# Selecting the 32 nearest of 64 through two sorted halves and a threshold, in a windowed-attention block on one core

## The reference

```python
diff = k_windows - q_h[:, :, None, :]
dist = jnp.sqrt((diff * diff * m_h).sum(axis=-1) + 1e-08)
dist = jnp.where(mask[None], dist, jnp.inf)
neg_d, loc = jax.lax.top_k(-dist, K)          # K = 32 of 64
infl = jnp.exp(-topd)                         # topd = -neg_d
infl = infl / (infl.sum(axis=-1, keepdims=True) + 1e-08)
context = jnp.einsum('btk,btkd->btd', infl, neighbor_v)
context = context + gate * 0.1 * heb_ctx      # a small per-head matrix on q / |q|
outs.append(q_h * context)
```

## Time and profile before

| | |
|---|---|
| median of three runs | 865.25 us (864.89 to 867.82) |
| the profiled execution | 865.7 us, span from first to last instruction 863.9 us |
| TensorE busy | 764.0 us, 88%; mean granted clock 0.895 of full speed |
| VectorE busy | 795.0 us, 92% |
| ScalarE busy | 620.0 us, 72% |
| GpSimd busy | 461.4 us, 53% |
| match_replace, all | 2048, 400.5 us, with 2048 value loads |
| max, all | 2048, 280.4 us |

### The profile page before, as it was taken

How to read it: one execution, slowest core, us unless ns; L and a number is a source line. 1 busy time by engine, 2 the same in 40 slices (tenths; PEclk the granted TensorE clock), 3 DMA queues, 4 the chain that set the end, 5 groups by cost and what they waited for, 6 DMA issues and landing times.

```text
span 863.9 us, 21621 instructions
## 1 busy us (share of the span) xinstructions
PE 764.0 (88%) x4885; PEld 500.8 (58%) x4885; DVE 795.0 (92%) x6746; ACT 620.0 (72%) x1862; POOL 461.4 (53%) x870
## 2 busy tenths in 40 slices
PE   5987999998899999888989988999889898989975
PEld 3444556565566665556666655666556666655644
DVE  5865999799999998999999999979999999999890
ACT  3982466687777876777877787668777777877763
POOL 1113455565556665556666665556555565666442
PEclk9995777799999987999999999779999999998775
DMA  5300000010000000011001110001010100110000
GB/s 164 106 21 16 23 18 25 21 30 28 29 29 29 26 27 27 29 30 30 25 28 30 31 30 28 28 21 31 27 30 29 30 30 23 31 31 29 23 9 10
DMA packets 49233, 27.27 MB, mean 32 GB/s; under 512 B 5513, under 2 KB 48593, under 8 KB 49105
## 3 DMA queue, kind: packets, MB, share of 16 engines
q1 hardware_dynamic: 49104, 25.90, 10.1%
HBM read 10.28 MB, written 4.19 MB: 17 GB/s over the span
## 4 chain that ended last, share of the span: by engine, by line
DVE 75%; PE 17%; ACT 3%; issue 2%; DMA 2%; POOL 1%; SPq 0%; POOLq 0%; ACTq 0%
DVE work L939 39%; DVE m L929 26%; DVE key L955 4%; PE psC L1167 2%; PE psD L1112 2%; PE psW L1183 2%; PE psD L1012 2%; PE psD L1104 1%; DVE den L972 1%; DMA big<-in_x 1%; PE psW L1185 1%; PE psW L1194 1%; PE psW L1136 1%; PE psX L1119 1%; PE psC L1095 1%
## 5 line engine op out<-in xcount | busy, mean ns | idle before, releaser
L939 DVE MATCH_REPLACE8 work<-m,work 128x64 f32<-128x64 f32 x1536 | 300.6, 204 | 0.0
L929 DVE MAX8 m<-work 128x8 f32<-128x64 f32 x1536 | 210.2, 205 | 0.0
L471 POOL TENSOR_TENSOR big<-work,con 128x512 f32<-128x512 f32 x128 | 161.7, 1286 | 21.5 <-ACT work L617 21.5
L1167 PE MATMUL psC<-vst,big 128*128 128x34 f32 x1024 | 139.6, 282 | 0.0
L1167 PEld LDWEIGHTS psC<-vst,big 128*128 128x128 f32 x1024 | 125.2, 193 | 17.1 <-issue 2.1
L450 POOL TENSOR_TENSOR hsc<-gat,rnn 128x8 f32<-128x8 f32 x64 | 13.0, 204 | 222.4 <-ACT rnn L699 222.4
L1136 PE MATMUL psW<-con,big 128*128 128x128 f32 x512 | 92.2, 309 | 27.8 <-POOL big L471 19.5
L939 DVE MATCH_VALUE_LOAD work<-m,work 128x8 f32 x1536 | 113.0, 74 | 0.0
L1136 PEld LDWEIGHTS psW<-con,big 128*128 128x128 f32 x512 | 62.5, 155 | 64.7 <-POOL big L471 46.7
L939 DVE MATCH_REPLACE8 work<-m,key 128x64 f32<-128x64 f32 x512 | 99.9, 203 | 0.0
L676 ACT ACTIVATE key<-key,bias 128x512 f32<-128x512 f32 x64 | 46.2, 722 | 55.2 <-DVE key L955 55.2
(11 more groups left out here) (204 smaller groups left out, 1630.9 us busy)
## 6 DMA issues: line engine op xcount, KB each, us to landing
hst<-hT_all SPq DMA_DIRECT2D x64, 96.0 KB
tst<-qT_all SPq DMA_DIRECT2D x256, 17.0 KB
big<-in_x SPq DMA_DIRECT2D x16, 256.0 KB, 2.8
xs<-in_x SPq DMA_DIRECT2D x64, 64.0 KB, 1.9
out<-yo SPq DMA_DIRECT2D x64, 64.0 KB, 1.6
sst<-nst SPq DMA_DIRECT2D x128, 3.0 KB
tst<-nst SPq DMA_DIRECT2D x128, 2.0 KB
con<-in_consts SPq DMA_DIRECT2D x1, 549.5 KB, 5.4
```

The source lines that it names most:

```text
L471: nc.gpsimd.tensor_tensor(wun[:, s, heads].rearrange("p h (v j) -> p h v j", v=2), work[:, s].rearrange("p (h j) -> p h j", h=NH)[:, heads ...
L929: last = v.max(m8[:, h], src[:, h * WIN:(h + 1) * WIN])
L939: last = v.match_replace(work[:, s, cols], m8[:, h], src[:, cols], GONE)
L1167: last = mm(pC[:, h * 2 * VD:(h + 1) * 2 * VD], wts[:, s, h], vst[:, s4, h].rearrange("p v e -> p (v e)"), start=True, stop=True)
```

## The change

The chunks, the stages and the layout of engines stay. What changes:

- **Distances.** The mask and product for a head are 160 columns wide (block before, 32 columns of q, own block); the two halves of a chunk are separate matmuls into partitions 0 to 63 and 64 to 127 (16 matmuls per chunk instead of 8; a float32 matmul is two instructions in the trace). One relu over 128 partitions replaces two over 64.
- **Selection.** VectorE works on the squared distances themselves. The 64 candidates of a head are paired, j with j+32: the minima of the pairs go to `low_high[:, 0]`, the maxima, negated, to `low_high[:, 1]`. Of each set of 32 the 16 largest are found in order (`pick`, `drop`, `pick`). Of two such lists `meet` takes the larger of one and the negated other, position by position, and `theta` is the minimum over positions: the threshold, which is the 33rd smallest distance.
- **Keep mask.** GpSimd subtracts (`diff` = key - theta, 512 elements), TensorE transposes `diff`, ScalarE takes two signs of it (with +1e-30 and -1e-30), and TensorE multiplies them with `count_bf`, a matrix that also counts equal distances ahead of a candidate, so that ties are resolved by position. VectorE multiplies (count >= -16) with the weights (`wsel`).
- **Weights.** TensorE transposes `key`, ScalarE takes log, exp(0.5 x), exp(-x) in the transposed layout (`infl`). GpSimd splits `wsel` by two masks (`wab`, two instructions of 512), which TensorE uses directly. The eight transposes of weights and the two copies `wts` go.
- **Values** are computed per block of 64 tokens and kept in `vst` for a batch; the copy of `hT_all` by DMA (`hst`) goes.
- **Order.** GpSimd: `diff`, `n_c` (moved from ScalarE), `sqs`, `sst`, `gat`, the mixing (four wide instructions instead of five), `wab`. One stage more in depth (i runs to 67). `keep_clock`, L1165 and `n2g` go; `selm` is computed once.

The diff, cut to its core:

```diff
-GONE = -1e4
+GONE = -3e38
+KEEP = -16.0
@@ gpsimd
-            def step(i, ph):
-                k, s, s4 = i - 2, ph % 2, (ph - 2) % 4
...
+            def step(i):
+                k = i - 1
+                if there(k):
+                    pool.wait_ge(theta_ready, k + 1)
+                    need(pool, dT_ready, k)
+                    nc.gpsimd.tensor_tensor(diff.rearrange("p (h j) -> p h j", h=NH),
+                                            key[:, k % 2].rearrange("p (h j) -> p h j", h=NH),
+                                            theta[:, k % 2].unsqueeze(2).broadcast_to([P, NH, WIN]),
+                                            ALU.subtract).then_inc(diff_ready, 1)
...
+                    nc.gpsimd.tensor_scalar(n_c[:, k % 2], x2[:, k % 2], nm_c[:, k % 2:k % 2 + 1], rs_c[:, k % 2:k % 2 + 1],
+                                            ALU.add, ALU.mult).then_inc(nc_ready, 1)
...
+                    nc.gpsimd.tensor_tensor(sqs[:], win, win, ALU.mult).then_inc(opnd_ready, 1)
...
+                    nc.gpsimd.tensor_tensor(t1[:].rearrange(h3, h=NH), cst[:, s, :, 0:HD],
                                             rden[:, s].unsqueeze(2).broadcast_to([P, NH, HD]), ALU.mult).then_inc(mix_step, 1)
...
+                k = i - 1
+                if there(k):
+                    pool.wait_ge(w_ready, k + 1)
+                    need(pool, c_ready, k - 1)
+                    for v, part in enumerate((of_own, of_before)):
+                        nc.gpsimd.tensor_tensor(wab[:, k % 2, v].rearrange("p (r t) -> p r t", r=4),
+                                                wsel.rearrange("p (r t) -> p r t", r=4),
+                                                part.unsqueeze(1).broadcast_to([P, 4, CH]), ALU.mult).then_inc(wab_ready, 1)
@@ scalar
+                    nc.scalar.activation(fst[:, 0], pDT, ACT.Sign, bias=bias[:, 4:5]).then_inc(f_ready, 1)
+                    nc.scalar.activation(fst[:, 1], pDT, ACT.Sign, bias=bias[:, 5:6]).then_inc(f_ready, 1)
...
+                    nc.scalar.activation(e, pXT, ACT.Ln, bias=bias[:, 1:2]).then_inc(ln_done, 1)
+                    act.wait_ge(ln_done, k + 1)
+                    nc.scalar.activation(e, e, ACT.Exp, scale=0.5).then_inc(root_done, 1)
+                    act.wait_ge(root_done, k + 1)
+                    nc.scalar.activation(e, e, ACT.Exp, scale=-1.0).then_inc(infl_ready, 1)
@@ vector
+            def pick(rnd, u):
+
+                where = slice(8 * rnd, 8 * rnd + 8)
+                for h in range(NH):
+                    last = v.max(top[:, u, h, where], low_high[:, u, h])
+                last.then_inc(picked, 1)
+
+            def drop(u):
+
+                for h in range(NH):
+                    last = v.match_replace(low_high[:, u, h], top[:, u, h, 0:8], low_high[:, u, h], GONE)
+                last.then_inc(picked, 1)
...
+                    v.tensor_tensor(low_high[:, 1], x4[:, :, 0], x4[:, :, 1], ALU.max).then_inc(pair_done, 1)
+                    v.tensor_tensor(low_high[:, 0], x4[:, :, 0], x4[:, :, 1], ALU.min).then_inc(pair_done, 1)
+                    dve.wait_ge(pair_done, 3 * i + 1)
+                    v.tensor_scalar(low_high[:, 1], low_high[:, 1], -1.0, None, ALU.mult).then_inc(pair_done, 1)
...
+                    v.scalar_tensor_tensor(out=e, in0=pB, scalar=0.0, in1=e, op0=ALU.max, op1=ALU.min).then_inc(d2_ready, 1)
...
+                    v.scalar_tensor_tensor(out=wsel, in0=pZ, scalar=KEEP, in1=infl[:, k % 2], op0=ALU.is_ge,
+                                           op1=ALU.mult).then_inc(w_ready, 1)
...
+                    v.scalar_tensor_tensor(out=meet, in0=top[:, 1], scalar=-1.0, in1=top[:, 0], op0=ALU.mult,
+                                           op1=ALU.max).then_inc(meet_done, 1)
+                    dve.wait_ge(meet_done, i + 1)
+                    need(dve, diff_ready, i - 1)
+                    v.tensor_reduce(theta[:, i % 2], meet, AX_X, ALU.min).then_inc(theta_ready, 1)
@@ tensor
+                    for r in range(4):
+                        last = nc.tensor.transpose(pDT[:, r * P:(r + 1) * P], diff[:, r * P:(r + 1) * P], ident)
+                    last.then_inc(dT_ready, 1)
...
+                    mm(pZ, count_bf[:, 0], fst[:, 0], start=True, stop=False)
+                    mm(pZ, count_bf[:, 1], fst[:, 1], start=False, stop=True).then_inc(count_ready, 1)
...
+                        for late in range(2):
+                            toks = slice(late * WIN, (late + 1) * WIN)
+                            last = mm(bank_of(r)[toks, g, 0:PW], tst[strip, s, g, toks], sst[strip, s, g, late * B0:late * B0 + PW],
+                                      start=False, stop=(g == NG - 1), skip_group_check=True)
-            def keep_clock(bank, times):
```

More of the change, by code:

```diff
@@ L54, in constants @@
     before = np.where(j > i, 0.0, BIG)
[L56 to L59, removed]
+    c[:, C_MASK:C_MASK + PW] = np.concatenate([before, np.zeros((P, QW)), own], 1)
+    slot = (np.arange(P) % WIN)[:, None]
+    tok = (np.arange(CH) % WIN)[None, :]
+    c[:, C_OWN:C_OWN + CH] = slot <= tok
+    c[:, C_OWN + CH:C_OWN + 2 * CH] = slot > tok
     e = np.arange(P) % 32
@@ L75, in constants, with counting, adaln_block @@
     return c
-def adaln_block(nc, x, encq, encv, w1, b1, w2, b2, base, hebu, hebv, dec, wr, amat, bmat, cin, wmod, consts, out):
+def counting():
+    jp, j = np.arange(WIN)[:, None], np.arange(WIN)[None, :]
+    eye, after = (jp == j).astype(np.float32), (jp >= j).astype(np.float32)
+    below, equal = 97.0 * eye - 1.0, 33.0 * eye - after
+    m = np.zeros((P, 2, P), np.float32)
+    for a in range(2):
+        rows = slice(a * WIN, (a + 1) * WIN)
+        m[rows, 0, rows] = 0.5 * (equal - below)
+        m[rows, 1, rows] = -0.5 * equal
+    return m
+def adaln_block(nc, x, encq, encv, w1, b1, w2, b2, base, hebu, hebv, dec, wr, amat, bmat, cin, wmod, consts, counts, out):
     ctx = ExitStack()
@@ L149, in adaln_block @@
         bsc = big[:].rearrange("p a s (b d) -> p (a s) b d", b=NB)
-        hst = sb("hst", [P, 2, 3 * WIN])
         tst = sb("tst", [P, 2, NG, CH])
         sst = sb("sst", [P, 2, NG, SW])
[L154 to L160, removed]
+        sqs = sb("sqs", [P, NG, 3 * WIN])
+        nst = sb("nst", [2 * NH, 2, 3 * WIN])
+        selm = sb("selm", [P, NB, NG, 2 * NH])
+        low_high = modn_all[:, 0:NH * WIN].rearrange("p (u h j) -> p u h j", u=2, h=NH)
+        top = gsgn_all[:].rearrange("p u (h n) -> p u h n", h=NH)
+        meet = gabs_all[:, 0].rearrange("p (h n) -> p h n", h=NH)
+        theta = sb("theta", [P, 2, NH])
+        diff = wmod_sb[:, 0:NH * WIN]
+        fst = sb("fst", [P, 2, 4 * CH], BF16)
+        infl = z8_all[:, 0:8 * CH].rearrange("p (s x) -> p s x", s=2)
+        wab = big[:, 0].rearrange("p s (v x) -> p s v x", v=2)
+        wsel = big[:, 1, 0, 0:4 * CH]
+        count_f = big[:, 1, 1, 0:2 * P]
+        vst = sb("vst", [P, NBLK, 4, VP])
         qh = sb("qh", [P, 4, NH, 2 * HD])
@@ L332, in steps, with there, new_blocks @@
                     routing(i)
-                step(i, i % 4)
-        def there(i, off):
-            return not isinstance(i, int) or 0 <= i + off < NCH
+                step(i)
+        def there(k):
+            return 0 <= k < NCH
         def column(k):
             return k * CH + (k // CPB) * WIN
+        def new_blocks(k):
+            c = k % CPB
+            return [2 * c + n for n in range(3) if n or c == 0]
         block = ctx.enter_context(nc.Block())
@@ L491, in step @@
[L491 to L496 removed]
+                    pool.wait_ge(mix_step, 4 * k + 4)
+                    nc.gpsimd.tensor_tensor(osp[:, s].rearrange(h3, h=NH), t1[:].rearrange(h3, h=NH), q,
+                                            ALU.mult).then_inc(osp_ready, 1)
@@ L506, in routing @@
                     pool.wait_ge(pG_ready, 2)
-            steps(pool, step, routing)
+            steps(step, routing)
         @block.scalar
@@ L727, in _ @@
+                k = i + 3
+                if there(k):
+                    act.wait_ge(pnn_ready, k + 1)
+                    need(act, gat_ready, k - 3)
+                    need(act, rnn_ready, k - 3)
+                    nc.scalar.activation(n2[:, k % 4], pNN, ACT.Copy, scale=-2.0).then_inc(n2_ready, 1)
+            steps(step, routing)
         @block.vector
```

703 lines of the change are left out of this document (360 added, 343 removed).

## The result

The changed kernel takes 991.97 us (median of 4 runs, 989.04 to 995.9), the kernel before, run beside it, 866.54: 1.144 times as long, 95% interval 1.137 to 1.151. Forecast were 907 us and a range of 750 to 950. The sign is right; the time lies 42 us outside the range.

A forecast was written before the change was run, and what follows sets the result against it. VectorE, waiting behind GpSimd for the shared port, was taken to bound the loop: start 92.5, loop 64 x 12.24 = 783.4 plus 6, tail 24, span 905.9; about 907 us, 4.8% slower, range 750 to 950.

The forecast's parts named there:

- the term for SyncE's queue: SyncE's DMA issues per step: one fewer (`hst`), nothing waits for it; no time added.
- from `key` to the next: Chain over TensorE and ScalarE between `key` instructions, 9.8 us a step, the bound if VectorE has no port stall.
- 12.24 us a step: VectorE's step in the loop with its waits behind GpSimd; 64 of them make 783.4 us.
- the forecast had allowed 6: Loop steps where TensorE is late at a slow clock: 6 us in all.
- Port stalls: VectorE's `meet`, pair maximum, minimum and negation wait behind GpSimd instructions: 3.5 us lost a chunk.
- the prediction's own balance, 11.58 us a step: Loop step at which the forecast sum equals the old kernel's time, so the change stops losing.
- VectorE's own work: VectorE per chunk without waits: 8.7 us, with 0.093 a max and 0.161 a replace with its load.
- the 11 us for swaps: ScalarE's time per chunk if each sign swapped tables; 8 us otherwise, both under 12.2.
- Start and tail: Outside the loop: start 90.5 + 2 = 92.5 us, tail 20.7 + 3.3 = 24 us.
- no port stall: Rival for the loop: VectorE not stalled, 9.8 us a step, 751 us in all; chance 0.22.
- Part of it: Rival: maximum waits for `wab`, minimum and negation slip in before `diff`; 10.6 us a step, 803 us; chance 0.14.
- TensorE becomes the bound: Rival: TensorE at 1.2 GHz, 14.5 us a chunk, about 1050 us, or 13.0 and 956; chance 0.09.

The follow-up runs named there:

- e1_rows_first: Changed kernel with SyncE issuing the norm rows before the output store: 848.71 us, ratio 0.975 to the kernel before.
- e5_store_mid: Changed kernel with the output store moved between the four `tst` loads and the norm rows on SyncE: 848.05 us, ratio 0.974.
- e6_xs_in_ring: Changed kernel with the `xs` load moved from behind the norm rows to between the store and the `tst` loads: 1032.32 us, ratio 1.184.
- b1_before_rows_first: Kernel before the change, with SyncE issuing the norm rows ahead of the store: 875.03 us, ratio 1.002.
- e9_diff_fillers_only: Changed kernel with only four unread matmuls added before TensorE's wait for `diff`, store still ahead of the norm rows: 982.32 us, ratio 1.130.
- e7_both_fillers: Changed kernel with norm rows first, two `tensor_reduce` for the pair instructions, and four unread matmuls before TensorE's wait for `diff`: 783.35 us, ratio 0.897.
- e3_fillers: Changed kernel with four unread 320-column matmuls before TensorE's wait for the norm rows: 964.09 us, ratio 1.107.

## Why the prediction failed, step by step

**The step that failed** is the term for SyncE's queue, which the prediction put at nothing: "SP issues one DMA less (`hst`); nothing waits for it" is true of `hst` and is all that it says of that queue's order. With it failed the ring "from `key` to the next" of 9.8 us. That ring was added up from TensorE and ScalarE only and closed over `key`. The real one closes over SyncE's queue, whose part alone is 6.7 us: the store 0.35, four loads 2.75, norm rows 1.18 and 1.10, the gaps between, and the landing. The rows stood in the trace of before; the prediction counted issues and didn't ask what stood first in the queue and how late it would be, though the change puts a logarithm and two exponentials, which wait for the transposes, ahead of `yo` on ScalarE. Shown: taking it out gives 143 us back (e1_rows_first, e5_store_mid), adding 0.47 us to it costs 40 (e6_xs_in_ring), and the exchange is worth nothing where there is no ring (b1_before_rows_first). The prediction had named this outcome as one that would refute it: a chain of waits that runs over ScalarE and TensorE.

**The forecast's 12.24 us a step** looks near the ring's 12.12. That is chance: the two have no term in common. What separates 907 from 992 in numbers is then the clock: 63 x (13.59 - 12.12) = 93 us, where the forecast had allowed 6. The trace bears this out: 57 x 1.60 = 91 us lie in TensorE's part of the ring. The reason for the 6 was that TensorE's busy time, 11.4 us at equal shares, fits under the step. (Its terms add up to 8.5 us or more, not 8.4, and 8.4 x 1.88 / 1.04 is 15.2, not 14.5; equal shares are then 11.8, still under 12.24. TensorE was busy for 656 / 63 = 10.4 us a step.) In a ring busy time is not the measure: each slow instruction of it lengthens the step, whatever pauses the engine has elsewhere. Once the ring is open (e1_rows_first, clock 0.83) the mean step is 0.15 us above the regular one, 10 us over the loop, about half of it in the first nine steps.

**Port stalls**: the mechanism was right, in kind and in place. With the ring open (e1_rows_first) the forecast's sequence can be read off:

```profile
406.92 0.18 DVE L1039 RECIPROCAL rden<-den 128x8 f32<-128x8 f32 x1
...
408.79 1.30 DVE L1062 SCALAR_TENSOR_TENSOR gabs_all<-gsgn_all 128x128 f32<-128x128 f32 x1
410.13 0.29 DVE L1066 TENSOR_REDUCE theta<-gabs_all 128x8 f32<-128x128 f32 x1
410.52 0.99 DVE L998 TENSOR_TENSOR modn_all<-key 128x256 f32<-128x256 f32 x1
411.44 1.26 DVE L999 TENSOR_TENSOR modn_all<-key 128x256 f32<-128x256 f32 x1
412.62 0.28 DVE L1001 TENSOR_SCALAR modn_all<-modn_all 128x256 f32<-128x256 f32 x1
```

`meet` stands behind `wab` 1, the maximum behind `wab` 2, the minimum behind `diff`. The picks start 5.9 us after `rden` (412.82), forecast were 6.87: the negation does not wait, because `n_c`, which was to stand in front of it, itself waits for ScalarE's `nm_c` and `rs_c` (it started at 412.67 there). 2.6 us are lost instead of 3.5 if the forecast's 3.3 for a free port is right (5.9 - 3.3; no run has a free port throughout), and the step is 11.23 us, not 12.24: even with all its stalls the selection is faster than the old one at 11.47. By the prediction's own balance, 11.58 us a step, the port alone would have made the change a gain. The Trainium skill ("SBUF — State Buffer", Who interferes with whom) says that on trn2 `tensor_reduce` never contends for the shared ports. By that rule the trace agrees: 693 and 680 ns for 512 elements, the rate of the earlier trace rows, beside GpSimd's work. The Trainium skill's page "VectorE: DVE Perf Modes", Rules for kernel authors, calls `tensor_reduce` the slowest operation and says to consider restructuring where it is on a hot path. Here it pays: the two take 0.69 and 0.68 us, the three instructions that they replace 0.98, 1.26 and 0.28. That is so only because of the stalls. At their shortest the three take 0.42, 0.42 and 0.28 us in the trace of the change, 1.1 in all against 1.37, so by these durations the reduces would be the slower way where nothing stalls.

**VectorE's own work**: 16 max took 1.50 us to the start of the next instruction (412.82 to 414.32 in e1_rows_first), 0.094 each (0.093 forecast), a replace with its load 0.16 (0.161). Both terms were right. **ScalarE**: a sign takes 0.69 to 0.70 us, and the trace has only three table loads, none of them in the loop; the 11 us for swaps did not come. **`wsel`** 0.61 to the next start, as forecast. **`wab` and `diff`** 1.29 and 1.21 us each (1.26).

**Start and tail**: +2 was forecast for the start, measured -0.5; +3.3 for the tail, measured +8.4 (cut at the first and last `key`; the forecast cut at the selection). With the loop these are the full balance: 905.9 forecast for the span, 988.3 measured.

**The rivals**: "no port stall", 751 us, was the right amount of gain in the wrong kernel; with the ring open, the pair stalls gone and the fillers in, 10.15 us a step was reached while `meet` still stalls for about 1 us. "Part of it" did not come: the minimum does stand behind `diff`. "TensorE becomes the bound" gave 956 to 1050 us and so held the measured time, but by TensorE's total work; TensorE is idle for 200 of the 856 us of the loop, and e9_diff_fillers_only shows that raising its clock outside the ring does little for the time. The time was in its band, the cause wasn't. None of the cases named a queue of DMAs.

**Left open**: why the clock falls in just these steps. No run held it at 2.4 GHz with the ring closed: fillers at two places brought 28 and 10 us, not the whole. From the reading of the 57 steps, 12.12 us and the 0.11 that the DMAs add in the mean, I estimate 12.2 us a step for such a kernel. Moving `yo` ahead of the logarithm and the exponentials on ScalarE, the other way to open the ring, was not tried.

## What to carry to other kernels

When a change makes one engine's result later (here `yo`, by half a step), look for it as the first wait of some in-order queue, SyncE's above all, and follow everything issued behind that wait to who needs it: a store that nobody waits for can hold up loads that everybody waits for. A queue's order can cost nothing in one kernel and 143 us in the next, so it is to be read again with each change of order elsewhere. A mechanism that is plain in the trace need not be what the time consists of: ask of each stall what would be waited for if it were gone, and of each ring whether a slow clock lies inside it.

## What the runs showed of the hardware

The waiting between VectorE and GpSimd goes in both directions. The minimum, 416 ns at its shortest, took 1258 ns in the median behind `diff`, and in e1_rows_first it ended 0.29 us after `diff` did. `diff` itself took 1.21 us in the mean beside the two-input maximum and minimum (the change and e1_rows_first) and 1.04 beside the reduces (e7_both_fillers). A pair reduction with `negate` does the work of a maximum and a negation in 0.68 us without a stall (669 to 695 ns over 64 of them in e7_both_fillers). The mean granted clock doesn't tell what a slow clock costs: the same kernel with the fillers at one place took 964 us at 0.782 (e3_fillers), with them at another 982 us at 0.796 (e9_diff_fillers_only). The second has the higher clock and is slower, because less of it was gained inside the ring.
